# Flamingo block on one core: the last batch and the last chunk of tokens take another way to the output

## The reference

```python
x = x + tanh(g_xattn) * attention(ctx, ctx, layernorm(x))     # 16 heads of 8, softmax over 1601 keys, dense layer
x = x + tanh(g_ffn) * ffn(layernorm(x))
# ffn: scores = sigmoid(x @ gate_W) * route_scale; the two largest of 8, divided by their sum, are the gates
#      h = gelu(x @ W1[e] + b1[e]);  y = sum_e gate[e] * (h[e] @ W2[e] + b2[e])
#      + gelu(x @ Ws1 + bs1) @ Ws2 + bs2
```

## Time and profile before

| | |
|---|---|
| median of 3 runs | 1310.46 us (1306.92 to 1322.75) |
| profiled execution | 1312.06 us, of which the trace spans 1310.3 us |
| TensorE, VectorE, ScalarE, GpSimd busy | 90%, 82%, 80%, 28% |
| mean granted clock of TensorE | 0.953 of 2.4 GHz |
| last Exp of the last step starts | 1257.13 us |

### The profile page before, as it was taken

The page is one execution under the profiler, slowest core; times in us unless marked ns, Lnnn a source line. Parts: engine busy times, 40 slices in busy tenths (PEclk is TensorE's granted clock), DMA queues, the critical chain, the costliest instruction groups (busy, mean ns, idle before and its releaser), DMA issues.

```text
span 1310.3 us, 30858 instructions
## 1 busy us (share of the span) xinstructions
PE 1183.9 (90%) x11995; PEld 455.4 (35%) x11995; DVE 1068.6 (82%) x1337; ACT 1049.8 (80%) x1962; POOL 372.3 (28%) x361
## 2 busy tenths in 40 slices
PE   2369899989999999999999999999999999999854
PEld 1123333333333433343334433343333433343223
DVE  8478888989889898989898898879898899989011
ACT  1017897989998899988998899878998899889931
POOL 7424041421425042422424042422424032000111
PEclk7558998999999999999999999999999999999977
DMA  5854452635464654626363655636373654400101
GB/s 133 201 120 94 103 113 62 142 76 123 96 139 94 134 120 101 138 66 130 80 150 77 139 118 104 132 73 123 75 155 77 139 118 104 87 13 26 43 15 49
DMA packets 64100, 133.71 MB, mean 102 GB/s; under 512 B 13769, under 2 KB 38034, under 8 KB 60882
## 3 DMA queue, kind: packets, MB, share of 16 engines
q1 hardware_dynamic: 63090, 130.95, 46.2%
q10 hardware_dynamic: 864, 0.79, 0.3%
HBM read 87.91 MB, written 43.40 MB: 100 GB/s over the span
## 4 chain that ended last, share of the span: by engine, by line
PE 75%; DVE 10%; DMA 6%; ACT 5%; issue 2%; POOL 1%; SPq 1%; ACTq 0%; POOLq 0%; DVEq 0%
PE o_ps L792 30%; PE a_ps L774 18%; PE b_ps L758 13%; DVE run_max L917 7%; PE a_ps L706 5%; DMA vctx<-ctx_t 3%; PE a_ps L702 3%; ACT probs L586 3%; PE b_ps L737 2%; PE a_ps L698 1%; PE b_ps L726 1%; PE a_ps L685 1%; ACT L601 1%; DMA q_op<-q_dram 1%; PE b_ps L740 1%
## 5 line engine op out<-in xcount | busy, mean ns | idle before, releaser
L917 DVE TENSOR_REDUCE run_max<-b_ps 128x2 f32<-128x1024 f32 x768 | 899.0, 1218 | 126.0 <-PE b_ps L758 118.2
L586 ACT ACTIVATE probs<-a_ps 128x512 f32<-128x512 f32 (+1 forms) x1664 | 901.9, 595 | 105.2 <-PE a_ps L774 90.8
L792 PE MATMUL o_ps<-probs,v_op 128*32 128x256 f32 (+1 forms) x5368 | 501.9, 445 | 1.4 <-ACT probs L586 0.6
L758 PE MATMUL b_ps<-k_op,q_op 48*128 48x512 bf16 (+1 forms) x2048 | 317.1, 342 | 43.5 <-DVE run_max L917 24.6
L774 PE MATMUL a_ps<-q_op,k_op 51*128 51x256 bf16 (+1 forms) x3328 | 327.8, 275 | 18.7 <-ACT probs L586 15.0
L774 PEld LDWEIGHTS a_ps<-q_op,k_op 51*128 51x128 bf16 (+1 forms) x3328 | 108.0, 96 | 347.1 <-ACT probs L586 302.7
L792 PEld LDWEIGHTS o_ps<-probs,v_op 128*32 128x32 f32 x5368 | 107.4, 108 | 186.2 <-issue 113.0
L758 PEld LDWEIGHTS b_ps<-k_op,q_op 48*128 48x128 bf16 x2048 | 87.1, 95 | 164.9 <-DVE run_max L917 93.3
L488 POOL TENSOR_TENSOR k_parts<-k_t,one 128x400 bf16<-128x400 f32 (+1 forms) x60 | 51.4, 856 | 182.8 <-ACT k_t L607 182.8
L499 POOL TENSOR_TENSOR rstd_q<-rstd_q,minus_half 128x4 f32<-128x4 f32 x8 | 8.7, 1085 | 290.3 <-DVE rstd_q L850 290.3
L528 POOL TENSOR_TENSOR attn<-num,den_all 128x256 f32<-128x256 f32 x16 | 11.7, 729 | 236.7 <-PE b_ps L758 151.8
(11 more groups left out here) (101 smaller groups left out, 612.0 us busy)
## 6 DMA issues: line engine op xcount, KB each, us to landing
k_op<-k_dram SPq DMA_DIRECT2D x64, 400.2 KB, 7.3
k_dram<-k_parts SPq DMA_DIRECT2D x32, 600.4 KB, 6.6
kctx<-ctx_t SPq DMA_DIRECT2D x16, 800.5 KB, 4.7
k_op<-k_dram SPq DMA_DIRECT2D x64, 200.1 KB, 7.8
vctx<-ctx_t SPq DMA_DIRECT2D x16, 800.5 KB, 11.0
o_dram<-o_s SPq DMA_DIRECT2D x32, 256.0 KB, 2.0
g_all<-g_dram SPq DMA_DIRECT2D x16, 512.0 KB, 6.0
k_dram<-k_parts SPq DMA_DIRECT2D x32, 200.1 KB, 5.8
```

The source lines that it names most:

```text
L586: act.activation(probs[0:keys, unit % PB, :], a_ps[at % AB][0:keys, :], ACT.Exp, scale=SCALE).then_inc(a_taken, 1)
L758: last = pe.matmul(slot[:, side, to:to + n_keys], q_op[buf][rows, p, 128 * t:128 * t + 128], k_op[buf][rows, p, k0:k0 + n_keys], start=Tru ...
L792: last = pe.matmul(o_ps[32 * j:32 * j + 32, cols], v_op[s // 2 % 2][0:KEYS[t], t, GP * (s % 2) + j, :], probs[0:KEYS[t], unit % PB, cols], ...
L917: dve.tensor_reduce(run_max[:, t, :, p, c:c + 1].rearrange("q v o -> q (v o)"), slot[:, :, :], AX.X, ALU.max).then_inc(b_taken, 1)
```

## The change

A function `last_steps` rewrites the order of the last steps, and the last batch and chunk get code of their own. An input `pick_in` (8 x 4 x 128, zeros and ones) is loaded at the start; the other input arrays are as before.

- Chunk 6's outputs (`Y`, `Z`) move from step 33 into step 31.
- Batch 15 isn't divided through DRAM. `OT` 0 (in step 31) and `OT` 1 (after the last `W`) transpose `o_s` on TensorE, four transposes each; VectorE inverts the sums of each token and multiplies into `attn_tok`; two transposes (`AT`), a copy by ScalarE, and the dense layer follow.
- The statistics of batch 14's tokens are taken as soon as these are there, and VectorE does the last normalisation in place of GpSimd (four `tensor_scalar`); GpSimd keeps the power.
- In the last chunk the hidden layers `FH` stand ahead of `FG` in the order.
- The last gates aren't spread through DRAM: for each hidden tile a matmul of `pick_s` and `g_t` puts them into a bank, VectorE multiplies `hid` by it, and the output matmuls add that tile to all four token tiles.
- The last output goes out as two DMAs.

```diff
+def last_steps():
+    c, b = CHUNKS - 1, BATCH - 1
+    during = ORDER[STEPS - 1]
+    during.insert(len(during) // 3, ("B", ("OT", 0, 0)))
+    for i in range(4):
+        at = len(during) * (9 + i) // 14
+        during[at:at] = [("Y", ("FY", c - 1, i)), ("Z", ("FY", c - 1, i))]
+    ORDER[STEPS] = [e for e in ORDER[STEPS] if e[0] in "VW"] + [("B", ("OT", 1, 0)), ("A", ("AT", b, 0)),
+                                                               ("B", ("D", b, 0))]
+    ORDER[STEPS + 1] = [("A", ("FT", c, 0)), ("A", ("FL", c, 0))]
+    ORDER[STEPS + 2] = [("A", ("FH", c, i)) for i in range(GELU_TILES + 1)] + [("A", ("FG", c, 0))]
...
+            def turn_outputs(h):
+                slot = b_slot(("OT", h, 0))
+                pe.wait_ge(o_copied, STEPS - 1 + h)
+                for i in range(2 * QTILES):
+                    cols = slice(SEQ * (i % 2) + 128 * (i // 2), SEQ * (i % 2) + 128 * (i // 2) + 128)
+                    last = pe.transpose(slot[:, 0, 128 * i:128 * i + 128], o_s[h][:, cols], ident[:, :])
+                last.then_inc(b_filled, 1)
...
+            def divide_tokens(h):
+                unit = b_ps[B_SLOT["OT", h, 0]][:, 0, :].rearrange("q (i j r) -> q i j r", i=4, r=32)
+                dve.wait_ge(b_filled, b_done("OT", h))
+                dve.reciprocal(sum_inv[:, :, :], unit[:, :, :, 16]).then_inc(inv_seq, 1)
+                dve.wait_ge(inv_seq, h + 1)
+                for side in range(2):
+                    last = dve.tensor_tensor(attn_tok[:, :, side, h], unit[:, side::2, :, DH * side:DH * side + DH],
+                                             sum_inv[:, side::2, :].unsqueeze(3).broadcast_to([128, QTILES, GP, DH]),
+                                             ALU.mult)
...
+            def last_normalise():
+                ...
+                for t in range(4):
+                    last = dve.tensor_scalar(xn["f"][:, t, :], x_s[:, 4 * c + t, :], mv["f"][:, t, 0:1],
+                                             rstd["f"][:, t:t + 1], ALU.subtract, ALU.mult)
...
+            def last_output():                                        # on TensorE
+                y = [b_ps[i // 2][:, i % 2, 0:128] for i in range(4)]
+                def spread(m):
+                    if m >= AB:
+                        pe.wait_ge(pick_taken, m + 1 - AB)
+                    pe.matmul(a_ps[m % AB][:, :], pick_s[HID:HID + EXPERTS, m, :], g_t, start=True,
+                              stop=True).then_inc(pick_filled, 1)
+                def grow(m):
+                    pe.wait_ge(pick_taken, m + 1)
+                    for i in range(4):
+                        last = pe.matmul(y[i], hid[:, m, toks[i]], w2_s[:, m, :], start=False, ...)
+                ...
+                spread(0)
+                for i in range(4):
+                    pe.matmul(y[i], hid_s[:, toks[i]], ws2_s[:, :], start=True, stop=False, ...)
+                spread(1)
+                for m in range(GELU_TILES):
+                    grow(m)
+                    if m + 2 < GELU_TILES:
+                        spread(m + 2)
...
+            def last_output():                                        # on VectorE
+                for m in range(GELU_TILES):
+                    dve.wait_ge(pick_filled, m + 1)
+                    dve.tensor_tensor(hid[:, m, :], hid[:, m, :], a_ps[m % AB][:, :], ALU.mult).then_inc(pick_taken, 1)
```

More of the change, by code:

```diff
@@ L155 @@
 ORDER[-2], ORDER[-1] = first_maxima()
+def last_steps():
[9 more added lines that the diff above has]
+    ORDER[STEPS + 2] = [("A", ("FH", c, i)) for i in range(GELU_TILES + 1)] + [("A", ("FG", c, 0))]
+    for s in range(STEPS + 3, LAST + 1):
+        ORDER[s] = []
+last_steps()
 def step_of(unit):
@@ L455, in _ @@
                     load_context("V", vctx, b + 1, vctx_in)
-                if s % 2 == 0 and 0 <= b - 1 < BATCH:
+                if s % 2 == 0 and 0 <= b - 1 < BATCH - 1:
                     spread_sums(b - 1)
-                if s % 4 == 2 and 0 <= (s - 6) // 4 < CHUNKS:
+                if s % 4 == 2 and 0 <= (s - 6) // 4 < CHUNKS - 1:
                     spread_gates((s - 6) // 4)
@@ L465, in _ @@
                     store_queries(sp, (s + 5) // 4)
-                if s % 4 == 1 and 0 <= (s - 9) // 4 < CHUNKS:
+                if s % 4 == 1 and 0 <= (s - 9) // 4 < CHUNKS - 1:
                     c = (s - 9) // 4
@@ L469, in _ @@
                     sp.dma_start(out[:, 4 * c:4 * c + 4, :], y_s[:, :, :]).then_inc(out_done, 16)
-            sp.wait_ge(out_done, 16 * CHUNKS)
+            for i in (0, 2):
+                sp.wait_ge(y_done, i + 2)
+                sp.dma_start(out[:, TILES - 4 + i:TILES - 2 + i, :], y_s[:, i:i + 2, :]).then_inc(out_done, 16)
+            sp.wait_ge(out_done, 16 * (CHUNKS + 1))
         @block.gpsimd
@@ L614, in aux_unit @@
                                                                                       t=t1 - t0, c=16), ACT.Copy)
+                elif kind == "AT":
+                    op = act.activation(attn[:, :], bank[:, 0:SEQ], ACT.Copy)
                 elif kind == "T":
@@ L685, in a_unit @@
                     last = pe.matmul(bank[:, :], wq_s[:, :], xn_t["q"][:, :], start=True, stop=True)
+                elif kind == "AT":
+                    pe.wait_ge(b_taken, b_done("OT", 1))
+                    for t in range(QTILES):
+                        last = pe.transpose(bank[:, 128 * t:128 * t + 128],
+                                            attn_tok[:, t].rearrange("q s h j d -> q (s h j d)"), ident[:, :])
                 elif kind == "FL":
@@ L723, in dense @@
                 slot = b_slot(("D", b, 0))
-                pe.wait_ge(attn_done, b + 1)
+                if b < BATCH - 1:
+                    pe.wait_ge(attn_done, b + 1)
+                else:
+                    pe.wait_ge(a_taken, a_done("AT", b))
                 for t in range(QTILES):
@@ L728, in dense @@
                 last.then_inc(b_filled, 1)
+            def turn_outputs(h):
[7 more added lines that the diff above has]
+                y = [b_ps[i // 2][:, i % 2, 0:128] for i in range(4)]
+                toks = [slice(128 * i, 128 * i + 128) for i in range(4)]
+                def spread(m):
[6 more added lines that the diff above has]
+                    for i in range(4):
+                        last = pe.matmul(y[i], hid[:, m, toks[i]], w2_s[:, m, :], start=False,
+                                         stop=(m == GELU_TILES - 1), skip_group_check=True)
+                        if m == GELU_TILES - 1:
+                            last.then_inc(y_filled, 1)
+                pe.wait_ge(a_taken, a_done("FG", CHUNKS - 1))
+                spread(0)
+                pe.wait_ge(b_taken, max(B_DONE.values()))
+                for i in range(4):
+                    pe.matmul(y[i], hid_s[:, toks[i]], ws2_s[:, :], start=True, stop=False, skip_group_check=True)
+                spread(1)
[3 more added lines that the diff above has]
+                        spread(m + 2)
             def ffn_output(c, i, half):
@@ L837, in fold_bias, with statistics @@
                 dve.wait_ge(bias_seq, 4)
-            def statistics(w, c):
+            def statistics(w, c, tiles=range(4)):
                 seq = lambda k: dve.wait_ge(bn_seq[w], 6 * c + k)
-                for t in range(4):
+                for t in tiles:
                     dve.bn_stats(stats[w][:, t, :], x_s[:, 4 * c + t, :]).then_inc(bn_seq[w], 1)
+                if tiles[-1] < 3:
+                    return
                 seq(4)
@@ L978, in _ @@
                     if kind in "SBZ":
-                        if s % 2 == 0 and 1 <= s // 2 <= BATCH and n == min(9, dense_at[0]):
+                        if s % 2 == 0 and 1 <= s // 2 < BATCH and n == min(9, dense_at[0]):
                             invert_sums(s // 2 - 1)
@@ L982, in _ @@
                             maximum(unit)
+                        elif unit[0] == "OT":
+                            divide_tokens(unit[1])
                         elif kind == "B":
                             add_dense(unit[1])
-                            if s % 4 == 0 and unit[1] >= 1:
+                            if unit[1] == BATCH - 2:
+                                dve.wait_ge(b_taken, b_done("D", unit[1]))
+                                statistics("f", CHUNKS - 1, range(2))
+                            elif unit[1] == BATCH - 1:
+                                dve.wait_ge(b_taken, b_done("D", unit[1]))
+                                statistics("f", CHUNKS - 1, range(2, 4))
+                                last_normalise()
+                            elif s % 4 == 0 and unit[1] >= 1:
                                 dve.wait_ge(b_taken, b_done("D", unit[1]))
```

30 lines of the change are left out of this document (25 added, 5 removed).

## The result

The changed kernel has a median of 1307.99 us over 20 runs, the kernel before 1315.69 us over 20. The ratio is 0.9937, interval 0.9916 to 0.9957: 8.3 us faster, where 17.0 were forecast, and outside the range of 1286 to 1303. The gain itself was also half of what I had summed up, and that part has causes. Two executions further down (the one of e3_filler and one of the six of e9_step31) had a mean granted clock of 0.78 and 0.74 over the whole kernel and took 1417 and 1451 us; no ratio and no comparison uses them.

A forecast was written before the change was run, and what follows sets the result against it. ScalarE was taken to bound step 31, and a chain of latencies the 50.7 us tail. Terms -3.9 + 9.0 + 1.4 - 1.0 - 1.1 + 12.6 = 17.0 us gave 1310.5 - 17.0 = 1293.5 us, range 1286 to 1303.

The forecast's parts named there:

- Gates by matmul, and the output: Copied gates to last addition: spreading on TensorE at full clock takes 8.6 us instead of 21.17, gaining 12.6 us.
- Rival 2: Half clock to the end through waits or pauses around FG: output 7.5 us more, gain 6.5, 1304 us; chance 0.14.
- Layers ahead of the gates: Last chunk, exponentials to copied gates: FG waits for five hidden layers, 6.95 us against 5.82, a loss of 1.1 us.
- Step 31: Chunk 6's four output tiles in this ScalarE-bound step become exposed and cost 3.9 us, bounds 0 and 4.9.
- Division through transposes: Copy of o_ps to end of dense addition: TensorE transposes replace the DRAM trip, 4.6 us against 13.60, 9.0 us gained.
- Statistics, normalisation, `FT` and `FL`: Dense addition to exponentials: earlier statistics and VectorE normalisation gain 1.4 us, half clock in FT and FL loses 1.0 us.
- Rival 1: Better covered: clock stays full in the tail or step 31's tiles hide; gain 20 to 24 us with both; chance 0.22.
- Rival 3: Slower: the clock already falls in step 31, where TensorE waits every period; up to 1315 us; chance 0.03.
- The base: Gain subtracted from the earlier kernel's three-run median, 1310.5 us, instead of its profiled execution of 1312.06 us.

The follow-up runs named there:

- e3_filler: Changed kernel with useless matmuls in TensorE's waits of the tail, spreading still over 8 rows; its one execution took 1417.41 us at a lowered clock.
- e9_step31: Changed kernel with chunk 6's tiles in tail pauses, 73-row spreads, reordered last chunk, useless matmuls in the tail and step 31; ratio 0.9824 to the kernel before.
- e1_rows: Changed kernel with the gate spreads contracting over 73 zero-padded rows instead of 8; copied gates to last addition 8.93 us instead of 15.45, execution 1308.8 us.
- e12_filler_again: Second run of the changed kernel with useless matmuls in the tail's waits and 8-row spreads; stretches 4.26, 6.14, 5.63 us, output 16.81 us.
- e6_filler_rows: Changed kernel with useless matmuls in the tail's waits and 73-row spreads; four tail stretches together 24.96 us instead of 36.59, execution 1290.16 us.
- e4_gates_first: Changed kernel with FG ahead of the five hidden layers again; exponentials to start of spreading 11.74 us instead of 7.93.
- e5_load: Kernel before the change with only the load of the 0/1 matrix added; ratio 0.998, interval 0.9958 to 1.0003.
- e2_pauses: Changed kernel with chunk 6's four output tiles moved from step 31 into the tail's pauses; step 31 30.16 us, then 5.12 and 7.12 us to the exponentials.

## Why the prediction was wrong

**The step that failed** is in "Gates by matmul, and the output": "Now on TensorE, at full clock after the layers", 8.6 us. It took 15.45. The price was right: at full clock the stretch takes 8.93 us (e1_rows, and 8.93 to 8.95 in five more traces). The clock was wrong, and the reason I gave for it, that dense matmuls after the layers hold it. It fell while TensorE had no pause, in a stretch in which matmuls over 8 of 128 rows take turns with others (e12_filler_again), and stayed with 73 rows in their place (e6_filler_rows). Rival 2 had the size (7.5 us more at half clock; 6.5 measured) but gave pauses as the cause and got 0.14. Its 1304 lies nearer to the measured time than the forecast does, for another reason than it gave. This step is 6.9 of the 9.1 us between forecast and measured sum.

**Layers ahead of the gates**: forecast a loss of 1.1, measured 2.1. The clock came back 4.3 us after the exponentials, not 2.4, 6.3 us into dense work, longer than the 5.3 that bounded my estimate. At full clock the stretch is 5.63, as the 5.6 in the text. That the order is worth having at all was argued there and is now measured: 3.8 us (e4_gates_first).

**Step 31**: forecast 3.9, measured 4.7 (33.57 against 28.86, again 33.56 in e6_filler_rows and 28.88 in e5_load). The mechanism was right, all of the surplus becomes idle time of ScalarE. The term was mis-sized: I took 1.11 us for a tile from a row where tiles follow each other. Between a pair and a half of values it holds TensorE for 1.31 us, as the timeline of the changed kernel shows, and 4 x 0.2 is the difference:

```profile
1250.72 0.94 PE L815 MATMUL b_ps<-w_s,hid 128*128 128x128 f32 x6
1251.49 0.39 PE L818 MATMUL b_ps<-w_s,hid 128*128 128x128 f32 x2
1251.71 0.39 PE L819 MATMUL b_ps<-ws_s,hid_s 73*128 73x128 f32 x2
1252.03 0.64 PE L870 MATMUL o_ps<-probs,v_op 128*32 128x256 f32 x8
```

That this part "buys nothing on the chain by itself" held: it cost 4.7. In the pauses the tiles cost less than they brought, since they kept the clock up for `OT` to dense layer: 5.12 us against 5.67, though 0.86 above the 4.26 of the same stretch at full clock without them (e2_pauses, e6_filler_rows).

**Division through transposes**: 9.0 forecast, 8.53 measured. The transposes already ran at half clock (1.09, not 0.63), which I had placed one step later. VectorE was quicker than I put it: reciprocal 0.26, both products 0.35 together.

**Statistics, normalisation, `FT` and `FL`**: a gain of 0.4 forecast, 0.13 measured. The gain at full clock was put a little low (1.4; 7.67 - 6.14 = 1.5 in e6_filler_rows), and what the half clock takes from it too (1.0; 7.54 - 6.14 = 1.4). The four instructions took 1.12, 0.28 each. That is below the 0.34 worked out at one value a cycle and close to the estimate of 0.29 from the Trainium skill, page "VectorE: DVE Perf Modes", section "Mode 2×_2P — use both read ports for one tensor"; no row here shows the same operation at the single rate. `FL` took 1.84 at half clock, near the 1.7 forecast.

**Rival 1** had as its argument that TensorE never idles for more than 4 us in the new tail. It idled 4.18 us ahead of `FT` (e1_rows and e4_gates_first have it too), but the clock had fallen 9 us before that wait ended, behind a wait of 0.59 us and within one of 0.89.

**Rival 3** had a chance of 0.03 and an argument against it that was false: "the clock is 1.00 all through that step". In six of the twelve traces of step 31 without added matmuls there (e3_filler left out), the clock fell to half near its start, for 3.4 us at a cost of 1.3 us, or for longer at a cost of 4.9. One trace without a fall had made me take that for a property of the step. The fall came in four of six traces with the tiles in step 31, in two of four with the tiles in the pauses, and in neither of the two with step 31 as in the kernel before. These are too few to say whether the change makes it more frequent, and with it a part of the 8.3 us stays open. The stretches in the table above are from two traces without a fall. That it comes where TensorE waits for the Exps is what the rows show; that filling these waits prevents it wasn't shown (e9_step31).

**The base.** I set the gain against the median of three runs. Over 20 it is 5 us higher, which alone would have moved 1293.5 to 1298.7. The rest of the way to 1307.99 is the gain that didn't come.

## What to carry to other kernels

Price each TensorE term of a new tail at both clocks, and look at the shape of the matmuls before assuming the higher one: this stretch with matmuls over 8 rows lost the clock as a pause does, and rows added with zero weights kept it at no cost (a spread takes 1.12 us either way at full clock). Work that is moved for cover belongs in the pauses of the chain that it is to shorten, not into a step whose bound engine hands every surplus on; and its price has to be read from a row in the same neighbourhood. Where the steady part of two executions differs by more than the edit is worth, compare stretches between two fixed instructions, not spans.

## What was unexpected of the hardware

- The granted clock fell from 1.00 to 0.50 with TensorE busy without a pause, and stayed at 0.50 to the end, some 12 us, while fp32 matmuls over 8 rows (2.07 us for 512 columns in two passes) took turns with ones over 128 rows. In all five traces with 8 rows, e3_filler's left out, it did so (15.42 to 16.81 us; e4_gates_first, where the spreads wait for the layers, 15.68 from there). In all six with 73 rows it stayed at 1.00 (8.93 to 8.95 us). Which property of the 8-row matmuls does it, the count of rows, their place or the data on them, wasn't told apart.
- In step 31, with TensorE busy for four fifths of the time, the clock fell in six of twelve executions, in the rest not.
- The other falls read here came in or soon after waits of TensorE (0.59 and 0.89 us around 1268 in the changed kernel, 1.08 us in step 31 of e12_filler_again); the returns read in the tails of the kernel before and the changed one came 3.4 to 6.3 us after TensorE's last wait had ended. The Trainium skill, page "TensorE: Matmul & The Clock Gate", section "HAM oscillation — how this bites in real kernels", says that bursts between waits are paid at the low clock; the trace agrees, with 5.1 us in this tail that filling the pauses gave back (e6_filler_rows, e12_filler_again).
